# Strassen's seven products for the down projection of a transformer block, with operand forms made on GpSimd

## What is computed

```python
gate_out = x_flat @ gate_w.T
up_out = x_flat @ up_w.T
hidden = jax.nn.silu(gate_out) * up_out
out_flat = hidden @ down_w.T
```

## Time and profile before

| | us |
|---|---|
| median of three runs (lowest, highest) | 1896.55 (1896.26, 1903.46) |
| the profiled execution, its own time | 1897.28 |
| its span, first to last instruction | 1895.5 |
| TensorE busy | 1823.7 |
| VectorE busy | 1134.5 |
| ScalarE busy | 771.0 |
| GpSimd busy | 504.8 |

### The profile page before, as it was taken

How to read it: one execution, slowest core, us unless ns; L and a number is a source line. 1 busy time by engine, 2 the same in 40 slices (tenths; PEclk the granted TensorE clock), 3 DMA queues, 4 the chain that set the end, 5 groups by cost and what they waited for, 6 DMA issues and landing times.

```text
span 1895.5 us, 27786 instructions
## 1 busy us (share of the span) xinstructions
PE 1823.7 (96%) x10592; PEld 891.2 (47%) x10592; DVE 1134.5 (60%) x2028; ACT 771.0 (41%) x1166; POOL 504.8 (27%) x999
## 2 busy tenths in 40 slices
PE   7989999999999988889999999999999999999997
PEld 4545655555556533334444444444444444444443
DVE  7877778678767764446445444656545444545555
ACT  5343444445434444345333343342453433334421
POOL 1354556446546555230000000202200000002214
PEclk9999999999999999999999999999999999999999
DMA  8443234324324396455222132449331322214201
GB/s 247 112 105 75 60 87 129 73 68 135 81 54 117 94 218 211 163 175 189 84 80 89 56 112 81 142 136 209 134 126 64 105 74 89 78 56 156 89 12 78
DMA packets 228020, 210.61 MB, mean 111 GB/s; under 512 B 183856, under 2 KB 184112, under 8 KB 227888
## 3 DMA queue, kind: packets, MB, share of 16 engines
q1 hardware_dynamic: 227024, 208.45, 38.1%
q10 hardware_dynamic: 864, 0.39, 0.1%
HBM read 133.03 MB, written 39.85 MB: 91 GB/s over the span
## 4 chain that ended last, share of the span: by engine, by line
PE 86%; DVE 5%; issue 2%; POOL 2%; SPq 2%; ACT 2%; DMA 1%; ACTq 0%; DVEq 0%; POOLq 0%
PE bank L868 34%; PE bank L883 20%; PE bank L774 19%; PE bank L822 4%; PE bank L786 3%; PE bank L810 3%; PE bank L833 2%; PE bank L789 1%; SPq L1354 1%; DVE row_max L1055 1%; POOL p_tiles L1234 1%; DVE xT_parts L1019 1%; DMA x_forms_spill<-x_parts 0%; DVE stats L1010 0%; ACT weight_forms L969 0%
## 5 line engine op out<-in xcount | busy, mean ns | idle before, releaser
L868 PE MATMUL bank<-x_forms,weight_forms 128*128 128x512 f16 x3136 | 702.6, 380 | 18.7 <-DVE up_blocks L1155 6.5
L868 PEld LDWEIGHTS bank<-x_forms,weight_forms 128*128 128x128 f16 x3136 | 306.1, 98 | 392.9 <-issue 14.0
L883 PE MATMUL bank<-w_down,hid 128*128 128x512 f16 x1792 | 408.3, 379 | 3.1 <-DVE hid L1172 3.1
L936 ACT ACTIVATE p_tiles<-bank 128x512 f32<-128x512 f32 (+1 forms) x352 | 193.2, 557 | 288.7 <-PE bank L810 285.0
L883 PEld LDWEIGHTS bank<-w_down,hid 128*128 128x128 f16 x1792 | 175.2, 98 | 215.0 <-DVE hid L1172 4.0
L1055 DVE TENSOR_REDUCE row_max<-bank 128x1 f32<-128x384 f32 (+3 forms) x352 | 219.6, 635 | 94.1 <-PE bank L789 93.1
L1260 POOL TENSOR_TENSOR acc<-acc,down_scale 128x1024 f32<-128x1024 f32 x16 | 38.9, 2431 | 765.3 <-DVE acc L1193 765.3
L774 PE MATMUL bank<-wq_parts,xT_parts 128*128 128x256 f16 x1536 | 217.7, 275 | 9.0 <-DVE wq_parts L1019 8.7
L1226 POOL TENSOR_SCALAR_AFFINE_SELECT p_tiles<-p_tiles 128x128 f32<-128x128 f32 (+2 forms) x352 | 137.8, 400 | 215.0 <-ACT p_tiles L936 214.3
L774 PE MATMUL bank<-wo_parts,att_parts 128*128 128x512 f16 x768 | 191.2, 381 | 2.0 <-DVE row L1104 1.4
L774 PEld LDWEIGHTS bank<-wq_parts,xT_parts 128*128 128x128 f16 x1536 | 144.3, 98 | 56.3 <-issue 13.9
(11 more groups left out here) (105 smaller groups left out, 1771.9 us busy)
## 6 DMA issues: line engine op xcount, KB each, us to landing
w_page<-gateT SPq DMA_DIRECT2D x56, 512.0 KB, 4.4
w_page<-upT SPq DMA_DIRECT2D x56, 512.0 KB, 4.6
w_page<-downT SPq DMA_DIRECT2D x56, 512.0 KB, 4.7
x_forms_spill<-x_parts SPq DMA_DIRECT2D x56, 256.0 KB, 2.5
att_spill<-att_made SPq DMA_DIRECT2D x64, 128.0 KB, 2.1
att_parts<-att_spill SPq DMA_DIRECT2D x16, 512.0 KB, 3.4
x_row<-x_spill SPq DMA_DIRECT2D x16, 512.0 KB, 3.5
out<-acc SPq DMA_DIRECT2D x16, 512.0 KB, 2.7
```

Source lines behind the costliest of these rows:

```text
L868: t = nc.tensor.matmul(strassen[bank_set(use)][to][:, :], w_form[:, use % 4, A_FORMS[a_form], k * P:(k + 1) * P], xF[:, :, B_FORMS[b_form] ...
L883: t = nc.tensor.matmul(to[:, :], hid[g % 2][:, c, a, i % 2, i // 2 * P:(i // 2 + 1) * P], w_down[:, g % 2 * GC + c, cols], start=g == grou ...
L936: nc.scalar.activation(p32[j][:, h0:h0 + heads, :], bank[5 + m % 2][:, 0:heads * n].rearrange("p (h c) -> p h c", c=n), ACT.Exp, scale=SCO ...
```

## The change

In the first ten rounds of a pass the down products are made by Strassen's scheme too. A round's hidden block is 2 x 2 (channel chunk by even or odd token tile) and its down weights are 2 x 2 (channel chunk by half of the outputs). For each of four pairs of tiles and each two rounds there are seven down products of four matmuls (two rounds, high and low part), in place of four products of eight matmuls. The last four rounds stay plain.

- PE: 28 down products of four matmuls per two rounds (L1028) in place of 16 of eight (L883). Plain ones are at L1015.
- Hidden forms: seven instead of four blocks per round. `hid_form` (POOL, L1416, L1418, L1421, L1425) makes S3, S1, S2 and S4 in float32 from `gate_blocks` and `up_blocks`, and each is split by `hid_hi` (now L1153) and `hid_lo` (now L1322).
- Weight forms: `d_form` (POOL, L1434) makes T1, T3, T2 and T4 of each round's down weights, in float16, each after the one before it.
- `acc` (now L1341, L1338) runs once per down product, so 28 times per two rounds instead of 16.
- The buffers of hidden blocks and down weights become a ring of three rounds' places, and the down scale, the row of x1 and the last product lie in free parts of it. A place is used again when the down products of the round three before are done.
- At the end of the attention the last head group's output goes to bank 3 instead of bank 7, weight pages are loaded once the scores are made (`scores_over`), and the first products stand ahead of an output projection.

The lines of the other pieces move: `w_form` L1148 to L1299, `sum` L1155 to L1306, `hidden` L1165 to L1316, products L868 to L997.

The diff, cut to its core:

```diff
-            for _ in range(4):
-                if DOWN_GROUPS[left[0][0]][-1] < n // 2:
+            for _ in range(10):
+                if left and DOWN_ROUNDS[left[0][0]][-1] < n:
                     down_at[left.pop(0)] = clock
-                    clock += one
+                    clock += one / 2
...
+        for f, form in enumerate(forms):
+            k = HID_PLAIN.index(form) if form in HID_PLAIN else None
+            before = [("hid_lo", n, forms[f - 1])] if f else []
+            if form in HID_MADE:
+                made = {"S3": [("hidden", n, 1)], "S1": [("hidden", n, 2), ("hid_form", n, "S3")], "S2": [("hid_form", n, "S1")],
+                        "S4": [("hid_form", n, "S2"), ("hidden", n, 3), ("hid_lo", n, "S3")]}[form]
+                put(PO, at[form] - 1.4, 1.35, "hid_form", n, form, after=made)
...
+        if w == 2 and c == 1 and not plain(r):
+            for k, form in enumerate(DOWN_MADE):
+                put(PO, at + 1 + 1.35 * k, 1.35, "d_form", r, form, after=[("w_cast", w, r, 0), ("w_cast", w, r, 1)] + (
+                    [("d_form", r, DOWN_MADE[k - 1])] if k else []))
...
+        ring = [sb(BB, f"down_forms{i}", [3 * NPR * HALF], F16) for i in range(3)]
...
+                        for r in rounds:
+                            on.wait_ge(s_hlo, lo_n(r, a_form))
...
+                            for a in range(2):
+                                t = nc.tensor.matmul(to[:, :], hid_f[r % NF % 3][:, HID_FORMS.index(a_form), a, pair * P:(pair + 1) * P],
+                                                     wd_f[r % NF % 3][:, DOWN_B[b_form], :], start=not added and r == rounds[0] and a == 0,
+                                                     stop=r == rounds[-1] and a == 1, skip_group_check=True)
...
+                elif kind == "hid_form":
+                    n, form = which
+                    _, to = hid_of(n, form)
+                    k = hform_n["hid_form", n, form]
+                    on.wait_ge(s_hid, 4 * n + {"S3": 2, "S1": 3, "S2": 3, "S4": 4}[form])
+                    if form == "S3":
+                        nc.gpsimd.tensor_tensor(to, gate_t[:, 0, :], gate_t[:, 1, :], ALU.subtract).then_inc(s_hform, 1)
...
+                elif kind == "d_form":
+                    n, form = which
+                    b = wd_f[n % NF % 3]
...
+                    nc.gpsimd.tensor_tensor(b[:, to, :], b[:, left, :], b[:, right, :], op).then_inc(s_dform, 1)
```

More of the change, by code:

```diff
@@ L44 @@
 X1_UP = 2.0 ** 8
[L47 removed]
+HID_BOUND = float(D) ** 2 / 2.0 ** 13
 MASKED = -1.0e30
@@ L449, in ffn_plan @@
                 put(VE, at, .78, "hidden", n, k, after=source + [("silu", n, k)] + before)
-                put(SC, at + .8, .65, "hid_hi", n, k, after=[("hidden", n, k)] + room)
-                put(VE, at + 1.5, .7, "hid_lo", n, k, after=[("hid_hi", n, k)])
-    for d, (q, m) in enumerate(downs):
+        if w == 0:
+            continue
+        at = {form: use_at[use] + (2.8, 7.4, 8.4, 10)[k] * one + .8 for k, form in enumerate(HID_PLAIN)}
+        at.update(S3=at["A21"] + 1.5, S1=at["A22"] + 1.5, S2=at["A22"] + 3, S4=at["A12"] + 1.5)
@@ new lines, in ffn_plan @@
+        forms, old = hid_forms(n), room_after(n)
+        room = [("down", *DOWN_LAST[old])] if old is not None else []
+        room += ([("acc", *DOWN_LAST[old])] if n >= NF else []) + (outputs if n > 1 else [])
+        for f, form in enumerate(forms):
[5 more added lines that the diff above has]
+                put(PO, at[form] - 1.4, 1.35, "hid_form", n, form, after=made)
+            put(SC, at[form], .65, "hid_hi", n, form, after=[("hidden", n, k) if k is not None else ("hid_form", n, form)] + room + (
+                [("hid_hi", n, forms[f - 1])] if f else []))
+            put(VE, at[form] + .7, .75, "hid_lo", n, form, after=[("hid_hi", n, form)] + before)
@@ L462, in ffn_plan @@
             room += [("out_store", tile - PT)] if p else []
         if part < ND - 1:
[L464 removed]
+            put(VE, at + one / 2, .72, "acc", q, m, after=[("down", q, m)] + room)
         else:
[L466 to L469 removed]
+            put(VE, at + one, 2.2, "acc", q, m, after=[("down", q, m), ("ds_scale", p), ("add_x1", tile)] + room + stats_free(plan, len(plan.norms)))
@@ L470, in ffn_plan @@
+        if part == ND - 2 and (q, m) == done_with(q, i):
+            put(PO, at + one + 1, 2.4, "scale_row", tile, after=[("acc", q, m), ("ds_scale", p)])
+            put(SY, at + one, .4, "last_x1", tile, moves=PAGE_MOVES, after=over + [("down", *DOWN_LAST[q - 1])] + (
+                [("add_x1", tile - 1)] if tile else []))
             put(VE, at + one + 5, 1.25, "add_x1", tile, after=[("scale_row", tile), ("last_x1", tile)])
-        if m % 2 and part == ND - 1:
+        if h and part == ND - 1:
```

300 lines of the change are left out of this document (198 added, 102 removed).

## The result

| | before | after |
|---|---|---|
| median of the runs, us | 1896.4 (1895.5 to 1903.5) | 1928.9 (1926.7 to 1932.5) |
| ratio, 95% interval | | 1.0165 (1.0136 to 1.0194) |
| profiled execution / its span, us | 1897.3 / 1895.5 | 1932.5 / 1930.7 |
| TensorE busy, matmuls | 1823.7, 10592 | 1814.4, 10432 |
| TensorE idle in the span | 71.8 | 116.3 |

The account below looks back on a forecast made before the run. TensorE was taken as the bound, busy 1823.7 of 1895.5 us. 1897.3 - 34.5 (gain) - 1.4 (start) + 49.6 (waits) + 11.2 (clock) = 1922.2, less 0.7 for the median: 1921.5 us, range 1866 to 1942.

Parts of the forecast that it names:

- the case called the forecast: Outcome case for the whole kernel: 1907 to 1938 us, chance 0.43.
- the likeliest side: Whole kernel slower by over 0.5%, chance 0.53, against 0.30 for faster and 0.17 for within 0.5%.
- the mechanism: VectorE instructions with two SBUF inputs and GpSimd instructions reading SBUF exclude each other for the whole instruction, delaying TensorE.
- The gain: Down products: 816 matmuls per pass in place of 896, 160 fewer over both passes at 0.216 us, 34.5 us saved.
- The walk through the critical place: Odd rounds' ends: turns with GpSimd make TensorE wait 5.7 us at eight places, 2 at two, 49.6 us together.
- t = 0: Walk's zero: when VectorE can start round 5's last `sum`, on `up_blocks`; TensorE was to start at 14.2 instead of 8.5.
- Behind round 9: End of round 9: no more weight forms and one down product more, so some 2 us of wait per pass.
- The start: Start of the feed-forward: earlier products and weight pages give -1.4 us, bounds -8 and +5.
- The clock: After waits, matmuls run at the lower clock: 1.4 us lost at eight places, 11.2 us, bounds 0 and 19.
- Even rounds: Ends of even rounds: no weight forms there, the walk ends 1 us early, so no wait was taken.
- `acc` and `sum`: Sign of being right: these VectorE instructions still take 0.69 us each.
- The gain comes through: Rival: exclusion costs VectorE but not TensorE, GpSimd coming in more loosely; 1862, up to 1885 us, chance 0.30.

Follow-up runs that it names:

- run 6: Kernel after, with the four hidden forms of a round on VectorE and weight forms still on GpSimd: 1892.6 us, ratio to before 0.9967.
- the other pairs: Old against new start: with weight forms on VectorE and `w_form` behind `sum`, 1891.6 and 1885.7 us; in the kernel after, 1935.8 and 1928.9 us.
- run 2: Kernel after, with a planner rule putting the next use's four `w_form` behind the `sum` TensorE waits for: 1897.9 us, ratio to before 1.0000.
- run 3: Kernel after, with the 80 weight forms on VectorE and hidden forms still on GpSimd: 1891.1 us, ratio to before 0.9959.
- run 4: Kernel after, with all forms, 80 weight and 80 hidden, on VectorE: 1889.8 us, ratio to before 0.9957.
- run 7: Kernel after, with all forms on VectorE and a rule putting `w_form` behind the next round's first `sum`: 1887.5 us, ratio to before 0.9937.
- run 10: Kernel after, with hidden forms on VectorE, weight forms on GpSimd and `w_form` behind `sum`: 1885.7 us, ratio to before 0.9931.
- run 12: Kernel after, new start kept, with weight forms on VectorE, hidden forms on GpSimd and `w_form` behind `sum`: 1885.7 us, ratio to before 0.9923.
- run 5: Kernel before, with only the change's new start of the feed-forward: 1891.3 us, ratio to before 0.9960.
- run 9: Kernel after, with weight forms T2 and T4 on VectorE; T1, T3 and the hidden forms stay on GpSimd: 1924.1 us, ratio to before 1.0128.

## Why the prediction was right, and where its terms were off

The time, 1928.9 us, lies in the range and in the case called the forecast; the likeliest side was right. The range says little: 1866 to 1942 holds every kernel of this study, from 1885.7 to 1935.8 us. What speaks for the prediction is the mechanism and its walk. Against the profiled execution the sum was +24.9 us and the measure is +35.2, of which 3.2 lie ahead of the feed-forward. By its own steps:

- **The gain**, 34.5 us. Right: 160 matmuls fewer, and where nothing is in the way (run 6) two rounds take 73.9 us instead of 76.0, close to the 72.6 of their matmuls.
- **The walk through the critical place.** Right in kind and nearly in size. With t = 0 at 1014.26 us it had the fourth `w_form` end at 8.2 (7.2 measured), the last `hidden` at 8.9 (7.8), the last `hid_lo` ahead of the `sum` at 13.5 (12.5) and TensorE start at 14.2 (13.3). The 0.9 is one turn that did not come: GpSimd began round 5's weight forms at -3.2 and not at -4.2, so the first `w_form` ended at 2.9, behind T4, and not at 3.9, behind S3; from there the walk keeps its step. A weight form took 1.15 us alone, and not the assumed 1.27, but mostly 1.48 beside VectorE. The estimate of 1.11 us from the 2.6 cycles an element of the Trainium skill (GPSIMD Engine Reference, section Elementwise — side-by-side cycle accounting) is the nearer one to the 1.15. Against 5.7 us for each of eight places stand 5.8, 4.7 and 4.3 in the first pass, 1.8, 4.7, 4.8 and 4.3 in the second, and at round 1 of the first pass 1.7 more than before: 32.2 for 45.6. Behind round 9 it was 4.1 and 5.2 us, not 2 each, since two `acc` come late there as well. Together 41.4 of the forecast 49.6.
- **The start**, -1.4 us. Mis-sized: -7.3 us alone, and -5 to -9 in the other pairs. The prediction's lower bound of -8 took it in. It cannot be seen in the trace of after, because the forms of round 1 take it back.
- **The clock**, 11.2 us with an upper bound of 19. This is the term that was off most: 25.2 us, or 22.4 without the part ahead of the feed-forward. From the second down product at round 5's end (1025.31 us) to the one at round 7's (1105.69) are 80.4 us, of which 72.6 are matmuls and 1.65 + 3.10 waits, so 3.0 us went to the lower level, 1.2 GHz, and not 1.4. From round 3's end to round 9's it is 2.5 us for each of three places, in both passes. Rows of TensorE in the kernel after:

```profile
947.85 1.04 PE L1028 MATMUL bank<-down_forms 128*128 128x512 f16 x2 [5.82 <-DVE down_forms L1322]
948.68 3.19 PE L997 MATMUL bank<-x_forms,weight_forms 128*128 128x512 f16 x8
```

```profile
1658.53 1.03 PE L1028 MATMUL bank<-down_forms 128*128 128x512 f16 x2 [3.11 <-DVE down_forms L1322]
1660.78 7.25 PE L997 MATMUL bank<-x_forms,weight_forms 128*128 128x512 f16 x24 [1.22 <-DVE gate_blocks L1306]
```

Eight matmuls took 3.19 us where 1.89 is the rule, and 24 took 7.25 where it is 5.34. The prediction took the lower of its two losses, 1.4 us for a wait of 3.38; the other, 2.4 us for one of 5.66, was the nearer. Why two waits of 3.1 and 1.2 to 1.7 us cost as much as one of 5.66 no run separates. Further, the last 256 down matmuls took 57.07 us after a wait of 2.48, where before they took 55.43 after one of 2.39.
- **Even rounds**: free, as said. **`acc` and `sum`**: 0.69 us, as said; `acc` came late only behind round 9, for which the prediction had no term (1.08 + 0.70 us in each pass).
- **The rivals.** "The gain comes through" named what decides it, VectorE and GpSimd coming in more loosely. Runs 2 to 4 go that way, and give 1890 to 1898 us and not 1862. So that rival's price was too good: run 4, without any turn but with 160 instructions more on VectorE, does not give the 34.5 us either. With all forms on VectorE the time against the kernel with the new start alone (spans 1887.3 and 1886.3) is +1.0 instead of -34.5. Of the 35.5 us, 8.5 are lost up to round 2, 11 in TensorE's idle time in the two steady stretches (325.1 and 323.9 busy of 330), some 8 in idle time at the passes' ends, and some 6 at the lower clock, 1.7 of it in the last down products; the rest, 2, lies ahead of the feed-forward, where the two spans differ anyway.

So against the profiled execution the forecast was 10.3 us too low: waits and start 3.7 us too high in idle time, the clock 14.0 too low. That the two partly cancel is luck.

Three kernels of this study (runs 7, 10 and 12, at 1887.5, 1885.7 and 1885.7 us) are faster than both kernels, by 0.6 to 0.8% against the one before. Of that, 0.4% is the start, which needs no Strassen down products (run 5).

## What to carry to other kernels

Work is not free because its engine is idle: on GpSimd, ask which VectorE instructions with both inputs in SBUF will stand beside it, and whether TensorE waits for one that is queued behind them. Try first to move a few such instructions past the deadline, before moving work between engines (run 2 won back 31 us with the same instructions on the same engines). Splitting the work over both engines at that place won back only 5 us here (run 9). Where a planner makes the orders, compare them after each move: runs 3, 4, 6 and 9 here changed the order together with the engine. And test the parts of a change apart: here a part worth 7 us was hidden under one that cost 36.

## What was not expected of the hardware

The two waits ahead of a stretch do not alone set whether it runs at the lower clock. TensorE's rows of two kernels that wait alike at two places; first the one with `w_form` behind `sum`:

```profile
1018.76 0.60 PE L1028 MATMUL bank<-down_forms 128*128 128x512 f16 x2 [0.99 <-DVE down_forms L1322]
1021.12 5.34 PE L997 MATMUL bank<-x_forms,weight_forms 128*128 128x512 f16 x24 [1.76 <-DVE gate_blocks L1306]
...
1094.36 0.60 PE L1028 MATMUL bank<-down_forms 128*128 128x512 f16 x2 [0.99 <-DVE down_forms L1322]
1096.72 7.03 PE L997 MATMUL bank<-x_forms,weight_forms 128*128 128x512 f16 x24 [1.76 <-DVE gate_blocks L1306]
```

and the one with write-only forms:

```profile
1014.24 7.03 PE L997 MATMUL bank<-x_forms,weight_forms 128*128 128x512 f16 x24 [0.69 <-DVE gate_blocks L1306]
...
1091.01 5.34 PE L997 MATMUL bank<-x_forms,weight_forms 128*128 128x512 f16 x24 [0.69 <-DVE gate_blocks L1306]
```

After the same 0.99 + 1.76 us the 24 matmuls took 5.34 us once and 7.03 the next time, and after 1.55 + 0.69 us 7.03 and then 5.34. Over both passes the slow value came at three of five such places in the first kernel and at one of five in the second. After 3.1 + 1.2 or 1.6 us, in the kernel after, it came at each place. So in this kernel the clock's term in a sum is a chance times 1.3 us or more, and a prediction should carry it as a range. What sets it stays open.
